# An attention and deformable-convolution kernel on one core: a dense half moved in front of the weighing, coordinates moved forward, and one GpSimd addition taken out between two gathers

## The reference

```python
# layer 0: attention over the 4096 pixels, 4 heads of 32 channels
xn = group_norm(x)                       # 32 groups
q, k, v = split(qkv_w @ xn + qkv_b)
o = softmax(q k^T / sqrt(32)) v
x = proj_w @ o + proj_b + x
# layer 1: modulated deformable convolution, 8 groups, 3 x 3 taps
offset_feat = conv1x1(concat(x, 2 * feat_s), W_off)
om = conv3x3(offset_feat, W_om) + b_om   # offsets y, x and mask per group and tap
val = bilinear(feat_s at pixel + tap + offset) * sigmoid(mask)
out = relu(conv(val, W_dcn) + b_dcn) + x
```

## Time and profile before

| | |
|---|---|
| median of 3 runs | 12684.2 us (12682.26 to 12689.32) |
| the profiled execution's own time | 12682.99 us |
| its span, first to last instruction | 12681.2 us |
| busy: PE, PEld, DVE, ACT, POOL | 73%, 40%, 57%, 37%, 81% |
| gathers on GpSimd | 7168, mean 998 ns |
| additions L465 on GpSimd | 13824, mean 250 ns |
| mean granted TensorE clock | 0.838 |

### The profile page before, as it was taken

How to read it: one execution, slowest core, us unless ns; L and a number is a source line. 1 busy time by engine, 2 the same in 40 slices (tenths; PEclk the granted TensorE clock), 3 DMA queues, 4 the chain that set the end, 5 groups by cost and what they waited for, 6 DMA issues and landing times. The chain is left out here.

```text
span 12681.2 us, 168047 instructions
## 1 busy us (share of the span) xinstructions
PE 9257.2 (73%) x56052; PEld 5057.7 (40%) x56052; DVE 7291.4 (57%) x10291; ACT 4747.5 (37%) x6104; POOL 10320.1 (81%) x21509
## 2 busy tenths in 40 slices
PE   4677778775778777776577777777577777777754
PEld 1244444442444444443244344444234444444444
DVE  4356566644666666664566666665456666666443
ACT  1344444432434434433244344343233434334322
POOL 0278888885788888888488888888858888888888
PEclk7888888886888888888788888888788888888876
DMA  1222211110011111111011111111101111111100
GB/s 48 77 67 70 66 23 24 24 24 23 21 33 25 24 24 25 25 24 29 13 25 33 24 24 25 25 23 24 28 16 31 25 25 25 25 23 24 24 22 21
DMA packets 373774, 373.51 MB, mean 29 GB/s; under 512 B 129440, under 2 KB 219936, under 8 KB 372768
## 3 DMA queue, kind: packets, MB, share of 16 engines
q0 software_dynamic: 229376, 235.34, 8.9%
q10 hardware_dynamic: 97920, 71.35, 1.8%
q1 hardware_dynamic: 45472, 54.53, 1.6%
HBM read 316.66 MB, written 44.04 MB: 28 GB/s over the span
## 5 line engine op out<-in xcount | busy, mean ns | idle before, releaser
L469 POOL DMA_INDIRECT g<-patches,idx x7168 | 7156.6, 998 | 1112.4 <-issue 949.5
L905 DVE TENSOR_REDUCE mx<-ring 128x2 f32<-128x1024 f32 x2048 | 2411.1, 1220 | 2919.3 <-PE ring L666 2381.8
L541 ACT ACTIVATE p<-ring 128x1024 f32<-128x1024 f32 x2048 | 1984.8, 1021 | 3832.3 <-PE ring L724 2960.3
L465 POOL TENSOR_TENSOR carrier<-carrier 128x1 f32<-128x1 f32 x13824 | 3063.5, 250 | 122.0
L708 PE MATMUL ps_x<-fx,hats 128*128 128x208 f32 x12288 | 2520.1, 356 | 120.4 <-DVE hats L1048 78.8
L721 PE MATMUL ring<-qf,kf 32*128 32x512 f32 x8192 | 1459.9, 786 | 1515.3 <-ACT hats L551 816.3
L708 PEld LDWEIGHTS ps_x<-fx,hats 128*128 128x128 f32 x12288 | 2192.2, 196 | 671.2 <-issue 598.1
L734 PE MATMUL ps_a<-p,v 128*64 128x512 f32 x4096 | 1442.3, 790 | 39.0 <-DVE shared L932 37.6
L734 PE MATMUL ps_b<-p,v 128*64 128x512 f32 x4096 | 1247.2, 692 | 0.0
L1067 DVE TENSOR_TENSOR ps_x<-ps_x,chosen 128x416 f32<-128x416 f32 x1024 | 611.1, 597 | 1053.2 <-PE ps_x L708 844.1
L574 ACT COPY vt<-ps_x 128x256 f32<-128x256 f32 (+1 forms) x512 | 204.5, 399 | 2659.1 <-PE ps_x L780 1505.9
(11 more groups left out here) (125 smaller groups left out, 7601.4 us busy)
## 6 DMA issues: line engine op xcount, KB each, us to landing
g<-patches,idx POOLq DMA_INDIRECT x7168
patch_in<-in_fpad ACTq DMA_DIRECT2D x544, 64.0 KB
patches<-patch_out ACTq DMA_DIRECT2D x136, 256.0 KB
fx<-in_fpad SPq DMA_DIRECT2D x20, 416.0 KB
p<-in_x SPq DMA_DIRECT2D x4, 2048.0 KB
xq<-in_x SPq DMA_DIRECT2D x32, 256.0 KB
fs_s<-in_fs SPq DMA_DIRECT2D x32, 256.0 KB
xs<-in_x SPq DMA_DIRECT2D x32, 256.0 KB
```

The costliest lines, as they stand in the source:

```text
L465: last = nc.gpsimd.tensor_tensor(carrier[:, col:col + 1], carrier[:, 0:1], carrier[:, 0:1], ALU.add)
L469: nc.gpsimd.indirect_dma_start(out=g[:, j, :], out_offset=None, in_=patches[b], in_offset=bass.IndirectOffsetOnAxis(ap=idx[:, t, j:j + 1], ...
L541: nc.scalar.activation(p[:, (2 * kt + pair) % 4, :, :], ring[slot][:, :, :], ACT.Exp, scale=SCALE)\
L905: V.tensor_reduce(mx[:, n:n + 2, c], ring[slot][:, :, :], AX.X, ALU.max).then_inc(ring_free[slot], 1)
```

## The change

- GpSimd: `RESTS` goes from 2 to 1. One addition stands in front of a gather where two stood; a part's first gather keeps only L440.
- TensorE: the dense half moves from behind the scores for the maximum to between the next tile's scores and the weighing. VectorE's `dense_half` moves in front of `maxima` likewise.
- TensorE: the distances move in front of `align` and `turn_part`, in every key tile but 0.
- ScalarE: `cut_hats` runs right behind `distances_to_hats`, one key tile earlier, behind `keep_turned` as before.
- Some names become general (`HATS` = 2, `WIDTHS`, `SLOTS`, `SLOT_TAPS`, `DENSE_CUTS`). With `DENSE_CUTS` = (0, 0, 0, 0, 2) the dense taps are turned in the last part, as before.

```diff
-RUN, RESTS = 1, 2
+RUN, RESTS = 1, 1
...
         def halves_at(s, kt):
-            return tuple((r, t, i, half) for half in range(2) for r, t, i in sets_with(s, kt, half))
+            return tuple((r, t, i, half) for half in (1, 0) for r, t, i in sets_with(s, kt, half))
...
# scalar, step
                         hand_queries(s + 1, uses, "queries")
-                    for r, t, i in weighed_at(s, kt):
-                        cut_hats(uses, t, i)
                     for r, t in aligned_at(s, kt):
                         finish_tile(tile_number(r, t))
...
                     for r, t, i in hats_at(s, kt):
                         distances_to_hats(uses, t, i)
+                        cut_hats(uses, t, i)
...
# tensor, align and turn_part
-                for tap in range(TAPS):
-                    last = mm(aligned, wdcn_s[:, tap, :], vt[:, tap, :], start=tap == 0, stop=tap == TAPS - 1)
+                for k, tap in enumerate(SLOT_TAPS):
+                    last = mm(aligned, wdcn_s[:, tap, :], vt[:, k, :], start=k == 0, stop=k == TAPS - 1)
...
-                if part == PARTS - 1:
-                    for d in range(DENSE):
-                        last = tr(turned[:, (picked + d) * 128:(picked + d + 1) * 128], dval[:, t % 2, d * C:(d + 1) * C],
-                                  ident_s[:, :])
+                for k, d in enumerate(range(DENSE_CUTS[part], DENSE_CUTS[part + 1]), picked):
+                    last = tr(turned[:, k * 128:(k + 1) * 128], dval[:, t % 2, d * C:(d + 1) * C], ident_s[:, :])
...
# tensor, step
                 for kt in key_tiles(s):
-                    maxima = maxima_at(s, last, kt)
+                    maxima, halves = maxima_at(s, last, kt), halves_at(s, kt)
                     if attends(s):
                         if 1 <= kt < KT - 1:
                             scores(s, uses, kt + 1)
                         if not last and kt == KT - 1:
                             max_to_rows(s + 1, uses, "rows")
+                    for r, t, i, half in halves[:1]:
+                        blocks_of_half(b, r, t, i, half, second)
+                    if attends(s):
                         weigh(s, uses, kt)
...
                         project(s - 1, uses)
-                    for r, t, i, half in halves_at(s, kt):
+                    if kt > 0:
+                        for r, t, i in hats_at(s, kt):
+                            distances(uses, r, t, i)
+                    for r, t, i, half in halves[1:]:
                         blocks_of_half(b, r, t, i, half, second)
                     for r, t in aligned_at(s, kt):
                         align(tile_number(r, t))
...
-                    for r, t, i in hats_at(s, kt):
-                        distances(uses, r, t, i)
+                    if kt == 0:
+                        for r, t, i in hats_at(s, kt):
+                            distances(uses, r, t, i)
...
# vector, step
+                    halves = halves_at(s, kt)
+                    for r, t, j, half in halves[:1]:
+                        dense_half(r, t, j, half)
                     if kt == 0 and projects(s - 1):
                         new_features(s - 1, uses)
                     for m in maxima_at(s, last, kt)[:1]:
                         maxima(uses, ("max", m), m)
-                    for r, t, j, half in halves_at(s, kt):
+                    for r, t, j, half in halves[1:]:
                         dense_half(r, t, j, half)
```

More of the change, by code:

```diff
@@ L41 @@
 CUTS = tuple(min(2 * part, PICKED - (PARTS - part)) for part in range(PARTS + 1))
-LAST_TAPS = CUTS[PARTS] - CUTS[PARTS - 1] + DENSE
+DENSE_CUTS = (0, 0, 0, 0, DENSE)
+WIDTHS = tuple(CUTS[part + 1] - CUTS[part] + DENSE_CUTS[part + 1] - DENSE_CUTS[part] for part in range(PARTS))
+SLOTS = tuple(sum(WIDTHS[:part]) for part in range(PARTS))
+SLOT_TAPS = tuple(tap for part in range(PARTS) for tap in (*range(CUTS[part], CUTS[part + 1]),
+                                                           *range(PICKED + DENSE_CUTS[part], PICKED + DENSE_CUTS[part + 1])))
+HATS = 2
 KT_TILE = KT // SUB
@@ L136, in build @@
         dpos = sb("dpos", [128, SUB, 3, UNITS])
-        hats = sb("hats", [128, 2, 1 + PAIRS, SET_GROUPS * 128])
+        hats = sb("hats", [128, HATS, 1 + PAIRS, SET_GROUPS * 128])
         chosen = sb("chosen", [128, UNITS, BLOCKS])
@@ L325, in build @@
         assert all(slots_in(o) % 2 == 0 for o in (FIRST, MID, LAST))
-        assert MID[-1][0] == "rows" and MID[0][0] == ("scores", 0)
+        assert ("rows", 2) in MID and MID[0] == (("scores", 0), 2)
         BATCH_SLOTS = USES_KV + slots_in(FIRST) + (STEPS_B - 2) * slots_in(MID) + slots_in(LAST)
@@ L547, in distances_to_hats @@
                 (slot,) = uses.slots(name)
-                made = hats[:, i % 2, :, :]
+                made = hats[:, i % HATS, :, :]
                 nc.scalar.activation(made[:, 0, :], ring[slot][:, 0, :], ACT.Abs, bias=plus_x, scale=-1.0)
@@ L571, in keep_turned @@
                 m = part_number(r, t, part)
-                width = 128 * (LAST_TAPS if part == PARTS - 1 else CUTS[part + 1] - CUTS[part])
+                width = WIDTHS[part] * 128
                 act.wait_ge(val_turned, m + 1)
-                nc.scalar.copy(vt[:, CUTS[part]:CUTS[part] + width // 128, :].rearrange("p k n -> p (k n)"), turned[:, 0:width]).then_inc(vt_ready, 1)
+                nc.scalar.copy(vt[:, SLOTS[part]:SLOTS[part] + WIDTHS[part], :].rearrange("p k n -> p (k n)"), turned[:, 0:width]).then_inc(vt_ready, 1)
             def step(s, b, i):
@@ L707, in blocks_of_half @@
                     for pair in range(PAIRS):
-                        last = mm(cells, hats[:, i % 2, 1 + pair, j * 128:(j + 1) * 128], fx[:, pair, :, group * GC:(group + 1) * GC],
+                        last = mm(cells, hats[:, i % HATS, 1 + pair, j * 128:(j + 1) * 128], fx[:, pair, :, group * GC:(group + 1) * GC],
                                   start=pair == 0, stop=pair == PAIRS - 1)
```

## The result

The changed kernel takes **13,907.5 us** (median of 3 runs, 13,903.2 to 13,908.7) against 12,684.2: ratio 1.0963 [1.0938, 1.0988], slower by 9.6%. The forecast was 13,600, with a range of 12,950 to 14,000. The span of the profiled execution is 13,906.9 us, 1225.7 more than before.

The account below looks back on a forecast made before the run. GpSimd bounds the kernel, TensorE 2% behind; after the change TensorE's order binds, 352 + 47 + 8 = 407 us a step. +1458 - 180 - 162 - 183 = +933 on 12,683 gives 13,600 us, range 12,950 to 14,000.

Parts of the forecast that it names:

- TensorE's own chain: A TensorE step in the kernel before without its waits for samples: 360.2 - 7.9 = 352 us.
- The half in front of the weighing: Odd key tiles: nothing fills the wait between maximum scores and next scores, 8.71 us for 6.68, +2.0 us.
- the clock's term: TensorE's half clock after idle gaps: six more slow rounds x 1.4 = 8 us a step, bounds 0 and 25.
- the forecast had 47: The new order's cost over a step's 28 tiles with maximum scores, without the clock: 47 us, bounds 30 and 55.
- The coordinates: Even tiles: turn and copy stand between distances and hats, 0.3 + 0.4 us; with the moved half, +2.0 us a tile.
- One addition: 82 us per tile: GpSimd: gather period from 1.47 to 1.32 us, 8.2 us less per tile, so 82 us for 90.
- the tail: Run's end, from the tenth tile from the end: 60 + 8 x 82 + 20 = 736 for 919 us, -183.
- the other end, 14: GpSimd's gain per tile if the mean addition of 250 ns went whole: 14 us; 8.2 was taken, as holds stay.
- Batch ends: Last step of each batch, without maximum scores, paced by GpSimd: three tiles at 82 us, -54 x 3 = -162 us.
- the sum of 933: Net change in us: slower steps +1458, waits for samples -180, batch ends -162, tail -183.
- the slow case: Slower as forecast, chance 0.72: 26.5 x 30 - 525 = +270 (12,950 us) to 26.5 x 75 - 525 = +1460 (14,140 us).
- the faster rival: GpSimd decides and the order costs TensorE nothing: steps fall to 352 us, 12,160 us in all; chance 0.13.

Follow-up runs that it names:

- Three additions: Kernel before with three GpSimd additions in front of a gather instead of two: 13,690.1 us, 1.0764.
- hats first: Kernel before, two additions, distances moved before align and turn, and on ScalarE the hats before the copy of turned samples: 12,704.9 us, 0.9988.
- the long addition: Kernel before with one addition of 88 bf16 columns in place of two of one column: 12,521.6 us, 0.9845.
- the half alone: Kernel before with only the dense half moved (TensorE between scores and weighing, VectorE before the maximum): two additions 13,966.6 us, 1.0982; one addition 17,150.2 us.
- the order: Changed kernel with the two additions put back, so only the order differs from the kernel before: 14,344.0 us, 1.1303.
- the filler: Changed kernel plus ten unread matmuls behind the maximum's scores in plain odd tiles: two additions 13,994.8 us, 1.1008; one addition 16,808.3 us.
- coordinates: Kernel before with only distances moved before align and turn, and the cut right behind its hats: two additions 12,743.3 us, 1.0028; one addition 16,376.7 us.

## Why the forecast came out as it did

**GpSimd is the bound, and TensorE stands 2% behind: right.** Three additions cost 973 us, hats first brought nothing, and the long addition brought the step to 354 to 356, near TensorE's own chain in the forecast (352). Its wait for samples fell to 14.7 us in six steps, from 40.6.

**The half in front of the weighing: right in mechanism.** The gap of 3.29 us between maximum scores and scores stands where it was put, and the half alone makes 76% of the order's price.

**The size of the clock's term: too small.** Counted over 26.5 steps, TensorE's longer busy time of 473 us, nearly all of it the clock, is 17.8 us per step; the forecast took 8, with bounds 0 and 25. A step grew by 52.3 us net; with the wait for samples that went (7.9) the order costs 60.2, 42.4 of it idle, where the forecast had 47, plus the clock's 17.8, where it had 8. Behind each of the two gaps of 2.5 to 2.8 us now stand scores and half, together 3.5 us of matmuls at full clock. The earlier trace rows show scores at full clock after such a gap, and I let that stand for most of them. It was the exception already: of the kernel before's 437 scores behind a gap of 2.4 to 3.0 us, 291 took longer than 1.3 us, for 1.14 at full clock. After the change 650 of 708 did, 359 more or 13 per step, so six further slow rounds were too few. The Trainium skill (TensorE: Matmul & The Clock Gate; Why this matters for your kernels) says that idle gaps between bursts bring the half clock back. The trace agrees in these counts, and so does the filler: with 0.73 us of idle left in the gap, the clock stays.

**The coordinates: small, as forecast, and hidden where they stand alone.** The forecast gave them 0.7 us per even tile, mostly turn and copy in front of the hats. Alone they cost 28 us in all: TensorE's slack of 2% under GpSimd takes them. On top of the moved half the difference is 1657 - 1252 - 28 = 377 us, 14 per step, or 1.0 for each of 14 even tiles. That order and half were timed on different chips leaves this figure rough; by the tiles' medians it is 0.5 to 0.6 (11.51 to 12.00 us in key tile 10, 13.06 to 13.66 in tile 24).

**One addition: 82 us per tile, right in the tail, where it counts (82.4).** The Trainium skill (SBUF — State Buffer; Who interferes with whom) says that a VectorE instruction with two SBUF inputs contends with a GpSimd instruction that reads SBUF. By that rule I took it that the holds stay, and the trace agrees in part: the mean addition is 253 ns for 250, and in the tail a tile's work shrank by 8.8 us, near the 8.2 of the forecast. In mid-run it shrank by 12.5, near the other end, 14: fewer gathers are held up (4 of 1118 took over 1.5 us, for 43 of 1356 before), and GpSimd stands idle instead, 508 us in five steps or about 100 a step for the 70 forecast. That gives no time back, since TensorE sets the pace there. The addition is also worth less at the ends than forecast. I let the first index of a batch's last step come 60 us in; it comes 82 us in (the step starts at 13,071, L445 follows at 13,153). The slowed order is only about 5 us of that: in the kernel before, too, VectorE writes that index (L1012) 76 to 77 us into the step. And the tail holds nine tiles, not eight: 82 + 9 x 82.4 + 12 = 836. Batch ends gave 104 us for 162, the tail 84 for 183. Of the 292 us by which the sum of 933 fell short, steps are 135, batch ends 58, the tail 99. Two slips in the working change little: three tiles at 82 after 60 us are 60 us less than 366, not 54, and the far end of the slow case adds 75 us a step where its bounds, 55 and 25, give 80.

**What the forecast took for certain and is not.** "1.47 to 1.32 is certain" was said for the faster rival. The period did fall, but in five of the six timings with the short period it brought late updates: the changed kernel took 2870 us more than in the first, the old order 3634 us more than with two additions. The forecast's number holds for the first measurement alone. That this one had no late update was luck: the forecast has no term for them, and the second measurement of the same kernel, 16,782 us, lies far outside its range. No row of the kernel before shows the danger. The old order with one addition, which by the forecast's own sums should come near 12,160, was timed once, and took 16,321.

**What stays open.** Why TensorE's updates come late when gathers are 1.34 us apart, no run tells. Five kernels with the short period (one addition, half, coordinates, the change, the filler) had them on two chips, and on the same two chips three kernels with two or three additions had next to none; so the additions do it, and the updates that come when a part's gathers end say the same. Whether by count or by spacing is not settled: the one long addition, which keeps the spacing, was timed on a third chip, and that might be as harmless as the first measurement was. Nor is it settled whether chip or hour made the first measurement harmless. The old order with one short addition and no late update was never seen, so the 12,160 stand untested.

## What to carry to other kernels

When a helper engine is the bound by 2%, everything done for it is worth at most these 2%, while an order change on the engine behind it can cost five times as much: look first at which piece of work fills each gap between writing a buffer and getting it back. A piece moved out of such a gap costs the gap and, behind it, the clock. Do not take out what spaces indirect DMAs on GpSimd without timing it on more than one chip: fewer but longer fillers kept the spacing here and gained 1.5%. And a time that meets the forecast once may do so by luck: the second measurement of this same kernel was a fifth higher.

## What the runs showed of the hardware

- With gathers issued every 1.34 us, semaphore updates of TensorE reached ScalarE and VectorE some 30 us late in the case shown (median 6.1 us in that run, waits of up to 58 us over all runs), in five kernels on two chips, and none was over 1.5 us late in the first measurement of the change; at 1.47 us or more such waits come to 0 to 130 us in whole executions. Nearly half of the late updates (44 to 47%) came within 2.5 us behind a part's last gather, for 2 to 5% of those in time. The Trainium skill (VectorE: DVE Perf Modes; The TRN2 errata) warns that high-rate semaphore increments of one engine can deadlock another and should be spaced. No run here shows a deadlock; that this lateness is a kin of it is not shown.
- The same kernel took 13,907 us in one measurement and 16,782 in another, while the kernel before, with two additions, differed by 0.3% between them.
- An idle gap of 2.4 to 3.0 us in TensorE is mostly followed by scores at the slow level (over 1.3 us for 1.14 in 650 of 708 such places of the changed kernel, 2.0 or more in 298 of them), and often by 3.3 to 3.8 us for a half that takes 2.38 (1.2 GHz for 2.4); with ten filler matmuls in the gap, 0.73 us idle, both kept their full rate.
- One GpSimd addition of 88 bf16 columns takes 0.34 to 0.35 us, as much as two of one column.
